# One LayerNorm application per batch in a transformer block with routed experts, the RMS factor moved into the q/k epsilon and into the copy of the values

## The chip, the cores and the metric

One Trainium2 chip, one of its cores. The metric is the device time of the program in microseconds (us); lower is better. The core has five engines that run their own instruction streams and meet at semaphores: TensorE (PE; its weight loads have rows of their own, PEld), VectorE (DVE), ScalarE (ACT), GpSimd (POOL) and SyncE (SP, which issues most transfers here).

## The reference

The input x is 8 batches of 512 tokens of 128 numbers. All is float32.

```
xn  = layernorm(x)                       # eps 1e-5
xr  = rms_norm(xn, ln1_w)                # eps 1e-6
q, k, v = xr @ Wq, xr @ Wk, xr @ Wv      # 16 heads of 8
q, k = q * rsqrt(sum(q*q) + 1e-6), same for k       # per head
a   = softmax over the later keys only of (q.k + rel_bias[bucket]) * scale
y   = (a @ v) @ Wo + xn
z   = relu(rms_norm(y, ln2_w) @ W1) @ W2 + y
x1  = x + layernorm(z)
out = x1 + layernorm(moe(layernorm(x1)))  # 8 experts, the best 2 of each token, inner size 352
```

A LayerNorm followed by an RMS norm without its weight is a LayerNorm scaled once more by a factor r of the token: xr = r * xn * ln1_w. The last token of a batch has no later key, so its attention weights are all equal and its row of a @ v is the mean of all values of the batch.

## The kernel before

The attention part runs over bodies b = 0 to 7, one for each batch, and each body has 20 positions n: four groups of four heads, five units of a group. In each position PE computes scores of a unit (`scores`, lines 684 to 694), ACT takes their exponential (`exp_unit`, line 947), and DVE or POOL multiplies them with the table of position biases (lines 414 to 422 and 1291). PE multiplies the result with the values (`pv01`, `pv23`, `pv4`, line 702). Into the same positions other work is written: the preparation of batches b+1 and b+2, and the output projection, the feed-forward layer, the norms and the routing of batches b-1 and b-2. Bodies 8 and 9 hold the rest of that work and the first expert tiles; then the expert tiles run alone, and a last stage adds and stores.

The order on each engine is written by hand. The tables `PE_AT`, `ACT_AT`, `DVE_AT` and `POOL_AT` give for each step the position at which its engine issues it, and within one position each engine's loop has a fixed order of steps. In the first dictionary of a table, a positive position of a preparing step means "in body b, for batch b+1", a negative one "in body b at position 20 + v, for batch b+2". Each engine works strictly in its order, so a step that waits holds everything behind it on its engine.

The preparation of a batch goes through one PSUM bank, M0, which has six uses per batch (`USES0 = 6`). PE fills it (`m0_full`), another engine empties it (`m0_free`), and `take0(b, k)` makes PE wait until use k-1 has been emptied:

- use 0: `pre_xt` transposes the normed x (line 618); ACT copies it to `XART` (line 953), with a sum over the tokens (`XSUM`)
- uses 1 and 2: `pre_qk` projects q and k (line 637); ACT copies them (line 959) and squares them (line 960)
- use 3: `pre_val` projects the values (line 643); ACT copies them into `V2`, which is laid out in blocks of 32 columns a head (lines 968, 969). PE at n = 1, ACT at n = 2
- uses 4 and 5: `pre_turn` transposes the normed q and k (line 650); ACT and PE split them into three bf16 parts (lines 1013 to 1021, 668), which SP sends to DRAM and reads back in the layout that `scores` needs. The first `pre_turn` stands at n = 4 on PE

Two applications of the norm are made on ACT, four instructions each (line 993): `xar` writes `XAR`, with the factor r included, for the projections (body b, n = 13, for batch b+2); `xa` writes `XA`, without it, for the residual (n = 1, for batch b-1).

DVE normalises q and k: `norm_sums` adds up the squares (line 1258) and adds the epsilon (line 1260), at n = 17 for batch b+2. `norm_roots` (lines 1266 to 1270) and `norm_apply` (line 1278) stand at n = 1, for batch b+1, and need the seeds that ACT makes at n = 1 (lines 976, 978). The order on DVE at the start of a body is: multiply of n = 19 (line 1291), `xb` (line 1552), multiply of n = 0 (line 414), the copy of the mean of values (`post(b, "vsum")`, line 1310), `norm_roots`, `norm_apply`, `post` of `o0` and `o1` (lines 1300, 1302, 1308), multiply of n = 2 (lines 421, 422), then `take_logits` (line 1336) and the routing (lines 1344 to 1357, in odd bodies only) or the multiply of n = 4 (line 1291). The order on PE is: `pv23`, `pre_val`, `vsum` (line 761), scores of n = 2, `pv4`, scores of n = 3, the transposes `rx` (line 785), `o0`, `o1` (line 758), scores of n = 4, `pv01`, `pre_turn` (line 650), `logits` (line 789), scores of n = 5, the first `peel` (line 668), `yt` (line 618) and so on. ACT has: exponentials of n = 0 and 1, seeds, `xa`, the copy `out1` (line 1027), exponential of n = 2, the two copies of values, the copy of `rx` (line 1034), exponential of n = 3, `xb2` (line 1138), exponential of n = 4, the first part (line 1013).

Of the kernel before, what the change touches and what calls it, by code (L numbers as in the profile page):

```python
# [25 lines left out]
P = 128  # L26
# [47 lines left out]
def block_kernel(nc, x_d, ln1_d, wq_d, wk_d, wv_d, rel_d, scale_d, wo_d, ln2_d, w1_d, w2_d,  # L74
# [26 lines left out]
    with ExitStack() as ctx:  # L101
# [8 lines left out]
        XA = sb("XA", [P, T, D])  # L110
# [11 lines left out]
        XAR = arena[:, WALL0 + 6656:WALL0 + 7168].rearrange("p (t c) -> p t c", t=T)  # L122
# [24 lines left out]
        XSUM = sb("XSUM", [P, NB])  # L147
# [22 lines left out]
        XBT = sb("XBT", [P, S])  # L170
# [82 lines left out]
        xar_rdy = sem("xar_rdy")  # L253
# [353 lines left out]
        def _(pe):  # L607
# [139 lines left out]
            def on_m1(body, k):  # L747
# [12 lines left out]
                elif k == "vsum":  # L760
                    mm = pe.matmul(M1[0:1, 0:P], XSUM[:, b:b + 1], WQKV[:, 2 * D:3 * D], start=True, stop=True)
# [177 lines left out]
        def _(act):  # L939
# [9 lines left out]
            def pre_copy(b, k):  # L949

                act.wait_ge(m0_full, USES0 * b + k + 1)
                if k == 0:
                    act.activation(XART[:, :], M0[:, :], ACT.Copy, accum_out=XSUM[:, b:b + 1]).then_inc(m0_free, 1)
                    return
                if k < 3:
                    if k == 1 and b >= 1:
                        act.wait_ge(ss_rdy, b)
                    ts = slice(2 * (k - 1), 2 * k)
                    act.activation(QK[:, ts, :], M0[:, :], ACT.Copy)
                    act.activation(SQ[:, ts, :], M0[:, :], ACT.Square).then_inc(m0_free, 1)  # L960
                    return
                if b == 0:
                    act.wait_ge(v2_const, 2)
                if b >= 2:
                    act.wait_ge(pv_done, 12 * (b - 1))
                v2 = V2[b % 2].rearrange("p t (n s) -> p t n s", s=64)
                v = M0[:, :].rearrange("p (t n a d) -> p t n a d", t=T, a=2, d=DH)
                act.activation(v2[:, :, :, 0:8], v[:, :, :, 0, :], ACT.Copy)
                act.activation(v2[:, :, :, 48:56], v[:, :, :, 1, :], ACT.Copy).then_inc(m0_free, 1)
# [19 lines left out]
            def norm(dst, b, r):  # L989
# [4 lines left out]
                return ins  # L994

            def xar(b):

                act.wait_ge(st_rdy, min(b, 1) + 1)
                if b > 0:
                    act.wait_ge(m0_full, USES0 * (b - 1) + 1)  # L1000
                norm(XAR, b, 1).then_inc(xar_rdy, 1)

            def xa(b):

                if b > 0:
# [75 lines left out]
            xar(1)  # L1081
# [718 lines left out]
```

## Time and profile before

| what | before |
|---|---|
| median of 3 runs | 620.87 us (619.76 to 622.0) |
| profiled execution, first to last instruction | span 616.4 us |
| what lies between them | 4.5 us, start and end of the program outside the span |
| PE busy | 528.4 us, 86% |
| ACT busy | 395.4 us, 64% |
| DVE busy | 384.0 us, 62% |
| POOL busy | 350.1 us, 57% |
| first exponential of bodies 0 to 7 at | 41.04, 77.06, 115.72, 155.76, 197.98, 240.65, 284.91, 327.74 us |

The profiled execution has no timed median of its own; its span is what the steps below are counted in, and a step that lengthens the span is taken to lengthen the median by as much. The busy shares are means over stages with different limits. A duration in a row is that of one instruction from issue to its end, and on ACT and DVE the next may start some 0.1 us before that end, so the pace is read from starts.

### The profile page before, as it was taken

The numbers are of one execution on the slowest core, as the hardware profiler recorded it, in microseconds if no ns is written. First come the engines' busy times: TensorE is split into PE (matmuls) and PEld (weight loads), VectorE is DVE, ScalarE is ACT, GpSimd is POOL, SyncE is SP. The second block draws the span as 40 slices with busy tenths as digits, with TensorE's granted clock in tenths as the row PEclk, the third lists the DMA queues.
The fourth block names the chain that finished last, engine by engine and source line by source line (L and its number), as shares of the span: only waits on it lengthen the run. The fifth ranks groups of instructions, "written<-read, shape, count | busy, mean of one in ns | idle before, by whom it ended". The sixth has DMA issues, their size and how long they took to land.

```text
span 616.4 us, 13926 instructions
## 1 busy us (share of the span) xinstructions
PE 528.4 (86%) x4585; PEld 387.8 (63%) x4585; DVE 384.0 (62%) x1089; ACT 395.4 (64%) x874; POOL 350.1 (57%) x448
## 2 busy tenths in 40 slices
PE   7868899899998899997898999989999599999170
PEld 5643455456565555654565667879899499999030
DVE  6745583965966839988658866446755335552047
ACT  3468988988878788777888783634544235554025
POOL 4023636555458875278965463764667766665535
PEclk9986999999999999999999999999999879999666
DMA  8756333203223232134546212110222122211074
GB/s 199 119 129 140 103 103 105 78 28 103 78 89 101 90 108 80 42 120 111 150 139 162 70 28 70 45 48 20 67 74 71 46 68 71 59 50 35 16 272 137
DMA packets 48118, 55.88 MB, mean 91 GB/s; under 512 B 7820, under 2 KB 42383, under 8 KB 45888
## 3 DMA queue, kind: packets, MB, share of 16 engines
q1 hardware_dynamic: 43728, 46.52, 27.7%
q0 software_dynamic: 4320, 8.47, 4.1%
q8 instruction: 39, 0.64, 0.4%
q14 instruction: 31, 0.25, 0.1%
HBM read 37.12 MB, written 18.29 MB: 90 GB/s over the span
## 4 chain that ended last, share of the span: by engine, by line
PE 42%; POOL 16%; DVE 15%; issue 11%; ACT 8%; DMA 5%; SPq 2%; DVEq 1%; POOLq 0%; ACTq 0%
PE OA L702 9%; POOL ytok L1696 8%; PE M L743 4%; PE SC L828 4%; PE M L779 3%; ACT arena L947 3%; PE SC L684 3%; POOL slots L1685 3%; POOL IDLE L1690 3%; PE OA L838 2%; PE SC L688 2%; PE M L618 2%; DVE SS L1258 2%; PE M L637 1%; PE SC L694 1%
## 5 line engine op out<-in xcount | busy, mean ns | idle before, releaser
L947 ACT ACTIVATE arena<-SC 128x1024 f32<-128x1024 f32 x160 | 161.7, 1039 | 13.3 <-PE SC L689 11.0
L828 PE MATMUL SC<-arena 128*128 128x128 f32 (+1 forms) x852 | 109.2, 279 | 0.9 <-DVE arena L1439 0.9
L828 PEld LDWEIGHTS SC<-arena 128*128 128x128 f32 (+1 forms) x852 | 101.6, 187 | 1.4 <-DVE arena L1439 1.1
L702 PE MATMUL OA<-arena 128*32 128x256 f32 (+1 forms) x1536 | 90.9, 356 | 6.7 <-DVE arena L422 2.8
L1685 POOL DMA_INDIRECT slots<-XBA,IDX x64 | 72.7, 1136 | 37.0 <-DVE IDX L1383 19.6
L1431 DVE TENSOR_TENSOR arena<-arena,SC 128x256 f32<-128x256 f32 (+1 forms) x142 | 43.5, 348 | 59.7 <-PE SC L828 49.0
L702 PEld LDWEIGHTS OA<-arena 128*32 128x32 f32 x1536 | 39.6, 110 | 46.2 <-issue 24.7
L838 PE MATMUL OA<-arena 128*128 (+1 forms) x426 | 61.1, 280 | 6.2 <-DVE arena L1431 4.2
L1696 POOL DMA_INDIRECT ytok<-YSA,XGA x39 | 40.5, 1039 | 42.9 <-POOL IDLE L1690 22.5
L421 POOL TENSOR_TENSOR arena<-arena 128x512 f32<-128x512 f32 x32 | 42.9, 1340 | 33.9 <-ACT arena L947 33.3
L838 PEld LDWEIGHTS OA<-arena 128*128 128x128 f32 (+1 forms) x426 | 54.4, 195 | 7.9 <-issue 7.9
L414 POOL TENSOR_TENSOR arena<-arena 128x512 f32<-128x512 f32 x23 | 31.2, 1358 | 45.1 <-ACT arena L947 45.1
L1044 ACT ACTIVATE arena<-SC 128x256 f32<-128x256 f32 (+1 forms) x142 | 38.6, 324 | 19.6 <-PE SC L828 14.2
L1439 DVE COPY arena<-arena 128x704 f32 x71 | 39.2, 553 | 17.4 <-issue 15.0
L1291 DVE TENSOR_TENSOR arena<-arena 128x1024 f32<-128x1024 f32 x32 | 40.3, 1261 | 14.7 <-ACT arena L947 14.7
L1696 POOL DMA_INDIRECT ytok<-arena x32 | 33.2, 1036 | 24.9 <-POOL IDLE L1690 20.2
L414 DVE TENSOR_TENSOR arena<-arena 128x512 f32<-128x512 f32 x41 | 34.1, 833 | 17.3 <-ACT arena L947 16.6
L688 PE MATMUL SC<-arena 72*128 72x384 bf16 x128 | 35.6, 332 | 7.9 <-ACT arena L947 7.9
L421 DVE TENSOR_TENSOR arena<-arena 128x512 f32<-128x512 f32 x32 | 28.3, 885 | 20.6 <-ACT arena L947 20.5
L684 PE MATMUL SC<-arena 72*128 72x512 bf16 x128 | 39.1, 388 | 1.3 <-ACT arena L947 1.3
L1050 ACT ACTIVATE YSA<-OA,XGA 128x128 f32<-128x128 f32 x39 | 14.3, 368 | 32.5 <-PE OA L838 17.7
L1662 POOL TENSOR_TENSOR arena<-arena,CF 128x512 f32<-128x512 f32 x16 | 20.3, 1286 | 22.8 <-ACT CF L1080 22.8
(238 smaller groups left out, 1073.8 us busy)
## 6 DMA issues: line engine op xcount, KB each, us to landing
arena<-parts SPq DMA_DIRECT2D x90, 192.0 KB
parts<-arena SPq DMA_DIRECT2D x16, 384.0 KB
arena<-ytok SPq DMA_DIRECT2D x8, 512.0 KB, 6.7
XGA<-slots SPq DMA_DIRECT2D x39, 65.0 KB
arena<-slots SPq DMA_DIRECT2D x32, 65.0 KB
X<-in_L_attn_x SPq DMA_DIRECT2D x4, 512.0 KB, 5.2
arena<-toe SPq DMA_DIRECT2D x16, 128.0 KB, 6.0
out<-X SPq DMA_DIRECT2D x8, 256.0 KB, 2.4
```

Of the source, the lines that this page charges most:

```text
L414: return eng.tensor_tensor(v, v, tab, ALU.mult)
L421: return [eng.tensor_tensor(a, a, TAB[:, h0:h0 + 3:2, P:3 * P], ALU.mult), eng.tensor_tensor(z, z, TAB[:, h0:h0 + 3:2, P:2 * P], ALU.mult)]
L684: mm = pe.matmul(s[:, 512 * i:512 * i + 512], KS[0:ROWS, h, 0:P], QS[0:ROWS, h, :], start=True, stop=True)
L688: pe.matmul(s[:, 512 * i:512 * i + 384], KS[0:ROWS, h, P:2 * P], QS[0:ROWS, h, P:4 * P], start=True, stop=True)
L702: mm = pe.matmul(OA[32 * j:32 * j + 32, q0:q0 + n], vals[:, t, 32 * h:32 * h + 32], probs(j), start=first, stop=last, skip_group_check=True)
L828: mm = pe.matmul(SC[0:n, r % 2, 512 * m + P * c:512 * m + P * (c + 1)], WSEL[s % 4][:, I * m + i0:I * m + i0 + n], XGT[r % 2], start=True, ...
L838: mm = pe.matmul(OA[:, 0:P], HTB[r % 2][0:n, P * c:P * (c + 1)], WALL[0:n, bass.ds(off + 2 * I + P * c, P)], start=c == 0, stop=c == NIC - 1)
L947: act.activation(EB[u], SC[:, n % 2, :], ACT.Exp).then_inc(exp_done, 1)
L1291: dve.tensor_tensor(e, e, TAB[:, heads, P:3 * P], ALU.mult).then_inc(mul_dve, 1)
L1431: ins = dve.tensor_tensor(HTB[r % 2][0:k, c0:c1], SGB[r % 2][0:k, c0:c1], SC[0:k, r % 2, 512 + c0:512 + c1], ALU.mult)
L1685: pool.indirect_dma_start(out=slots_d.ap(), out_offset=bass.IndirectOffsetOnAxis(ap=IDX[b // 2 % 2][:, k, T * r + t:T * r + t + 1], axis=0 ...
L1696: pool.indirect_dma_start(out=ytok_d.ap(), out_offset=bass.IndirectOffsetOnAxis(ap=XG[r][:, D + 1:D + 2].bitcast(I32), axis=0), in_=YS[r], ...
```

## The change

`xa` and `xar` become one step, made at the place of `xar` (n = 13, for batch b+2): ACT writes `XA[b % 3]`, without r, into one of three buffers, and both the projections and the residual read it. The projections of q, k and v are then short of the factor r. For q and k, (r q) * rsqrt(sum((r q)^2) + eps) is the same as q * rsqrt(sum(q^2) + eps / r^2), so `norm_sums` adds an epsilon of the token that `x_roots` computes (three more small DVE instructions in each of its two calls). For v, the copy from PSUM into `V2` multiplies by r; it leaves ACT and becomes the DVE step `values`, two `tensor_tensor` instructions a batch, at n = 2 of DVE's table, which in the loop is behind DVE's multiply of n = 2. The sum over tokens in `XART`'s copy goes away; the sum of the values for the last token (`vsum`) is now made by PE from `V2` with eight matmuls against a column of ones instead of one against `XSUM`. `XBT` shares the memory of `ZT`.

```
-ACT_AT = (dict(val=2, seed=1, ..., xar=-7, xa=1),
-    dict(..., xa=3))
-DVE_AT = (dict(norm0=-3, norm1=1, norm2=1, lg=2, ...
+ACT_AT = (dict(seed=1, ..., xa=-7), dict(...))
+DVE_AT = (dict(val=2, norm0=-3, norm1=1, norm2=1, lg=2, ...
...
             def pre_xt(b):
                 take0(b, 0)
-                pe.wait_ge(xar_rdy, b + 1)
-                turn4(M0, XAR).then_inc(m0_full, 1)
+                pe.wait_ge(xa_rdy, b + 1)
+                turn4(M0, XA[b % 3]).then_inc(m0_full, 1)
...
                 elif k == "vsum":
-                    mm = pe.matmul(M1[0:1, 0:P], XSUM[:, b:b + 1], WQKV[:, 2 * D:3 * D], start=True, stop=True)
+                    pe.wait_ge(m0_free, USES0 * b + 4)
+                    v = V2[b % 2].rearrange("p t (n s) -> p t n s", s=64)
+                    for t in range(T):
+                        for i, at in enumerate((0, 48)):
+                            mm = pe.matmul(M1[0:1, 64 * i:64 * i + 64], ONES[:, 0:1], v[:, t, :, at:at + DH],
+                                           start=t == 0 and i == 0, stop=t == T - 1, skip_group_check=True)
...
                 if k == 0:
-                    act.activation(XART[:, :], M0[:, :], ACT.Copy, accum_out=XSUM[:, b:b + 1]).then_inc(m0_free, 1)
+                    act.activation(XART[:, :], M0[:, :], ACT.Copy).then_inc(m0_free, 1)
                     return
...
-                act.activation(v2[:, :, :, 0:8], v[:, :, :, 0, :], ACT.Copy)
-                act.activation(v2[:, :, :, 48:56], v[:, :, :, 1, :], ACT.Copy).then_inc(m0_free, 1)
...
+            def xa(b):
+
+                act.wait_ge(st_rdy, min(b, 1) + 1)
+                if b >= 3:
+                    act.wait_ge(*drained(b - 2, "wo"))
                 for t in range(T):
                     i = T * b + t
-                    ins = act.activation(dst[:, t, :], X[:, i, :], ACT.Identity, bias=NM0[:, r, i:i + 1], scale=RSR[:, r, i:i + 1])
+                    ins = act.activation(XA[b % 3][:, t, :], X[:, i, :], ACT.Identity, bias=NM0[:, 0, i:i + 1], scale=RSR[:, 0, i:i + 1])
+                ins.then_inc(xa_rdy, 1)
...
+                link(dve.tensor_tensor(u, a, y[:, 0].unsqueeze(1).broadcast_to([P, 2, n]), ALU.mult))
+                dve.tensor_tensor(y[:, 1], y[:, 1], u[:, 0], ALU.mult)
+                link(dve.scalar_tensor_tensor(NM0[:, 1, i0:i1], u[:, 1], KQ_EPS, y[:, 0], ALU.mult, ALU.mult))
...
-                dve.tensor_scalar(SS[:, :], SS[:, :], KQ_EPS, None, ALU.add).then_inc(ss_rdy, 1)
+                ss = SS[:, :].rearrange("p (t c) -> p t c", t=T)
+                dve.tensor_tensor(ss, ss, NM0[:, 1, T * b:T * (b + 1)].unsqueeze(2).broadcast_to([P, T, 2 * H]), ALU.add
+                                  ).then_inc(ss_rdy, 1)
+
+            def values(b):
+
+                dve.wait_ge(m0_full, USES0 * b + 4)
+                if b == 0:
+                    dve.wait_ge(v2_const, 2)
+                if b >= 2:
+                    dve.wait_ge(pv_done, 12 * (b - 1))
+                v2 = V2[b % 2].rearrange("p t (n s) -> p t n s", s=64)
+                v = M0[:, :].rearrange("p (t n a d) -> p t n a d", t=T, a=2, d=DH)
+                r = RSR[:, 1, T * b:T * (b + 1)].unsqueeze(2).unsqueeze(3).broadcast_to([P, T, H // 2, DH])
+                dve.tensor_tensor(v2[:, :, :, 0:8], v[:, :, :, 0, :], r, ALU.mult)
+                dve.tensor_tensor(v2[:, :, :, 48:56], v[:, :, :, 1, :], r, ALU.mult).then_inc(m0_free, 1)
...
                     if b < NB and (n % UNITS in (0, 2, 4) or n % UNITS == 1 and takes(b, n // UNITS)):
                         dve.wait_ge(exp_done, NU * b + n + 1)
                         mul(b, n)
                     if 1 <= due(PRE["norm0"], b, n) < NB:
                         norm_sums(due(PRE["norm0"], b, n))
+                    if 1 <= due(PRE["val"], b, n) < NB:
+                        values(due(PRE["val"], b, n))
                     if 1 <= due(PRE["norm1"], b, n) < NB:
                         norm_roots(due(PRE["norm1"], b, n))
```

## Rows read from the trace of the kernel before

**Rows 1.** Busy time by engine in body 3 and in its middle; then granted clock

```profile
155.76:197.98 42.22, 39.87 (x384) 24.98 (x384) 31.06 (x88) 35.32 (x64) 25.28 (x27) 1.00 0.28 90
...
166.50:192.50 26.00, 25.96 (x248) 16.93 (x247) 17.17 (x50) 20.34 (x39) 15.25 (x16) 1.00 0.28 91
```

**Rows 2.** Chain of waits, body 3: start, us, what; first and last of 51 pieces

```profile
164.84 0.59 PE M L650 x4
...
191.29 1.07 PE M L637 x4
```

**Rows 3.** Timeline of DVE into body 3: start, us, what, idle before

```profile
155.01 1.91 DVE L1258 TENSOR_REDUCE SS<-arena 128x128 f32<-128x1024 f32 x1 [0.62 <-ACT arena L960]
...
162.36 1.43 DVE L1278 TENSOR_TENSOR arena<-arena,RSQ 128x256 f32<-128x256 f32 x4
...
166.26 0.41 DVE L422 TENSOR_TENSOR arena<-arena 128x256 f32<-128x256 f32 x1
166.60 0.17 DVE L1336 COPY LG<-M 128x32 f32<-128x32 f32 x1
```

**Rows 4.** Timeline of PE at the same place in body 3

```profile
163.76 1.07 PE L702 MATMUL OA<-arena 128*32 128x256 f32 x16
164.77 0.66 PE L650 MATMUL M<-IDN,arena 128*128 128x128 f32 x4
```

**Rows 5.** Timeline of ACT at the same place in body 3

```profile
158.16 1.64 ACT L993 ACTIVATE XA<-X,NM,RSR 128x128 f32<-128x128 f32 x4
...
160.13 0.60 ACT L1027 ACTIVATE OS<-OA 128x512 f32<-128x512 f32 x1 [0.33 <-PE OA L702]
...
161.53 0.39 ACT L968 ACTIVATE arena<-M 128x256 f32<-128x256 f32 x1
...
162.06 0.63 ACT L1034 ACTIVATE XBT<-M 128x512 f32<-128x512 f32 x1
```

**Rows 6.** Instruction groups by line: count | busy us, mean ns | idle before

```profile
L1266 DVE TENSOR_TENSOR NWA<-RSQ 128x128 f32<-128x128 f32 x8 | 2.3, 292 | 1.0 <-ACT RSQ L978 0.7
```

**Rows 7.** Timeline, PE's L650 and DVE's slot, in the first and last of six bodies

```profile
84.55 0.66 PE L650 MATMUL M<-IDN,arena 128*128 128x128 f32 x4
...
87.38 1.21 DVE L1291 TENSOR_TENSOR arena<-arena 128x1024 f32<-128x1024 f32 x1
...
295.57 0.66 PE L650 MATMUL M<-IDN,arena 128*128 128x128 f32 x4
...
297.85 0.17 DVE L1336 COPY LG<-M 128x32 f32<-128x32 f32 x1
```

**Rows 8.** Timeline of body 5: PE's output projection, and DVE's take of it

```profile
253.81 1.05 PE L770 MATMUL M<-WO,YT 128*128 128x128 f32 x8
...
256.01 0.69 DVE L1314 TENSOR_TENSOR Y<-M,XA 128x512 f32<-128x512 f32 x1
```

**Rows 9.** Timeline of PE: `vsum`, and the nearest chain of 64-column matmuls

```profile
158.57 0.38 PE L761 MATMUL M<-WQKV,XSUM 128*1 128x128 f32 x2
...
170.25 1.90 PE L795 MATMUL M<-MM,ONES 128*128 128x64 f32 x16
```

**Rows 10.** Timeline of DVE at the start of the program

```profile
16.69 1.90 DVE L1258 TENSOR_REDUCE SS<-arena 128x128 f32<-128x1024 f32 x1 [1.16 <-ACT arena L960]
...
19.57 0.29 DVE L1266 TENSOR_TENSOR NWA<-RSQ 128x128 f32<-128x128 f32 x1 [0.72 <-ACT RSQ L978]
```

**Rows 11.** Timeline of PE around its longest wait between 70 and 480 us

```profile
413.45 0.93 PE L838 MATMUL OA<-arena 128*128 x6 [2.49 <-DVE arena L1431]
...
414.33 2.64 PE L828 MATMUL SC<-arena 128*128 128x128 f32 x12
...
418.07 1.49 PE L828 MATMUL SC<-arena 128*128 128x128 f32 x12
```

**Rows 12.** Busy time by engine, as rows 1, behind two waits of PE

```profile
414.50:417.90 3.40, 3.40 (x18) 3.40 (x18) 2.14 (x7) 0.99 (x4) 2.55 (x3) 0.50 0.27 80
...
46.00:56.00 10.00, 9.86 (x66) 4.05 (x66) 7.31 (x11) 7.08 (x9) 2.51 (x2) 0.50 0.76 140
```

More of the change, by code:

```diff
@@ L46 @@
     dict(rx=0, logits=1, vsum=0, count=3, o0=1, o1=2, yt=3, wo=5, zt=6, h0=7, h1=7, h2=7, h3=7, ffn_a=8, ffn=8))
-ACT_AT = (dict(val=2, seed=1, xt=-6, qk0=-5, qk1=-2, out0=12, out1=1, rx=2, rexp=6, yt=4, ysq=12, zt=7, h0=8, h1=9, h2=10, h3=10, xb2=3, part0=4, half0=4, last0=6, part1=8, half1=9, last1=10, xar=-7, xa=1),
-    dict(out1=0, rx=0, xb2=2, rexp=3, yt=4, zt=6, ysq=6, h0=6, h1=6, h2=7, h3=7, xa=3))
-DVE_AT = (dict(norm0=-3, norm1=1, norm2=1, lg=2, top2=3, top2b=3, vsum=0, o0=1, o1=1, wo=4, ffn=13, astat=13, place=5, place2=6, tab0=6, tab1=6, tab2=9, ln=16, xstat=16, xb=19),
+ACT_AT = (dict(seed=1, xt=-6, qk0=-5, qk1=-2, out0=12, out1=1, rx=2, rexp=6, yt=4, ysq=12, zt=7, h0=8, h1=9, h2=10, h3=10, xb2=3, part0=4, half0=4, last0=6, part1=8, half1=9, last1=10, xa=-7),
+    dict(out1=0, rx=0, xb2=2, rexp=3, yt=4, zt=6, ysq=6, h0=6, h1=6, h2=7, h3=7))
+DVE_AT = (dict(val=2, norm0=-3, norm1=1, norm2=1, lg=2, top2=3, top2b=3, vsum=0, o0=1, o1=1, wo=4, ffn=13, astat=13, place=5, place2=6, tab0=6, tab1=6, tab2=9, ln=16, xstat=16, xb=19),
     dict(lg=1, top2=1, top2b=2, vsum=0, place=3, place2=3, tab0=4, tab1=17, tab2=21, o0=1, o1=2, wo=5, ffn=8, astat=9, ln=12, xstat=13, xb=15))
@@ L109, in block_kernel @@
         X = sb("X", [P, NT, D])
-        XA = sb("XA", [P, T, D])
+        XAS = sb("XAS", [P, 2, T, D])
         WALL0 = 22528
@@ L169, in block_kernel @@
         XB = [XBA[:, r] for r in range(2)]
-        XBT = sb("XBT", [P, S])
+        XBT = ZT
         R = 2 * T
@@ L952, in pre_copy @@
                 if k == 0:
-                    act.activation(XART[:, :], M0[:, :], ACT.Copy, accum_out=XSUM[:, b:b + 1]).then_inc(m0_free, 1)
+                    act.activation(XART[:, :], M0[:, :], ACT.Copy).then_inc(m0_free, 1)
                     return
[L955 to L967, printed above, removed]
-                act.activation(v2[:, :, :, 0:8], v[:, :, :, 0, :], ACT.Copy)
-                act.activation(v2[:, :, :, 48:56], v[:, :, :, 1, :], ACT.Copy).then_inc(m0_free, 1)
+                if k == 1 and b >= 1:
+                    act.wait_ge(ss_rdy, b)
+                ts = slice(2 * (k - 1), 2 * k)
+                act.activation(QK[:, ts, :], M0[:, :], ACT.Copy)
+                act.activation(SQ[:, ts, :], M0[:, :], ACT.Square).then_inc(m0_free, 1)
             def root_seeds(b):
@@ L1068, in _ @@
             x_seeds(0)
-            xar(0)
-            for k in range(4):
+            xa(0)
+            for k in range(3):
                 pre_copy(0, k)
@@ L1080, in _ @@
             act.activation(CF[:, :], CF[:, :], ACT.Exp).then_inc(tab_exp, 1)
-            xar(1)
+            xa(1)
             for k in range(2):
@@ L1110, in _ @@
                             third_part(due(PRE[f"last{m}"], b, n), m)
-                    if 2 <= due(PRE["xar"], b, n) < NB:
-                        xar(due(PRE["xar"], b, n))
+                    if 2 <= due(PRE["xa"], b, n) < NB:
+                        xa(due(PRE["xa"], b, n))
                     for k, name in enumerate(("xt", "qk0", "qk1")):
@@ L1309, in post @@
                 elif k == "vsum":
-                    dve.tensor_scalar(VROW[0:1, :], M1[0:1, 0:P], 1.0 / S, None, ALU.mult).then_inc(free1(body, k), 1)
+                    dve.tensor_scalar(VROW[0:1, :].rearrange("p (n a d) -> p a n d", a=2, d=DH),
+                                      M1[0:1, 0:P].rearrange("p (a n d) -> p a n d", a=2, d=DH), 1.0 / S, None, ALU.mult
+                                      ).then_inc(free1(body, k), 1)
                     dve.wait_ge(*drained(body, k))
@@ L1314, in post @@
                     dve.tensor_tensor(Y[:, :, :].rearrange("p t d -> p (t d)"), M1[:, :],
-                                      XA[:, :, :].rearrange("p t d -> p (t d)"), ALU.add).then_inc(free1(body, k), 1)
+                                      XA[b % 3].rearrange("p t d -> p (t d)"), ALU.add).then_inc(free1(body, k), 1)
                 elif k == "ffn":
@@ L1451, in _ @@
             norm_sums(0)
+            values(0)
             norm_roots(0)
```

24 lines of the change are left out of this document (2 added, 22 removed).

## The prediction

> **What bounds the kernel now.** I read the page's busy shares first, then the bodies one by one as stretches, then the chain of waits inside a body, and last the timelines of each engine around the place where the changed steps stand. The shares name no bound: PE 86%, ACT 64%, DVE 62%. By body they say more. In body 3, 42.22 us long, PE is busy 39.87, ACT 35.32, DVE 31.06, and from 166.5 to 192.5 us PE is busy in 25.96 of 26.00 us [rows 1]. The chain of waits says the same: from the first `pre_turn` (line 650) to the q projection (line 637) it runs on PE alone, in 51 pieces without a wait for another engine [rows 2]. Only around the boundary of two bodies does it leave PE, for ACT (exponentials and copies). So a body is a PE-bound stretch of some 27 us, and a boundary of some 13 us in which ACT, DVE and PE wait for each other. Work taken from ACT can only count in the boundary; a delay put in front of PE's `pre_turn` counts in full.
>
> At the boundary DVE is the fullest engine. In body 3 its row starts at 155.01, on ACT's last square, and runs without idle time past 166.60 [rows 3]. PE meanwhile reaches its first `pre_turn` at 164.77, right behind `pv01` [rows 4]. Before the change that is no conflict: `pre_turn` needs the normed q and k, which DVE has finished at 163.8, four instructions from 162.36 [rows 3], and the free bank, which ACT has emptied with its two copies (line 968 at 161.53, the next step at 162.06) [rows 5].
>
> **What leaves ACT.** The four instructions of `xa` take 1.64 us, of which the next may overlap 0.1; the two copies 0.53 (161.53 to 162.06) [rows 5]. The accumulator read I leave at nothing. That is 2.1 us a body, 15 us in seven bodies, and 1.5 more in body 8. I count it at nothing. With `xa` in place ACT already waits 0.33 us for PE's `pv4` before it copies `OS` [rows 5]; without `xa` it waits 1.9. The two copies let `XBT` start 0.53 us earlier, but what follows from that (the transposes `o1`, then DVE's `post`) ends in DVE's queue, which is full. In the middle of the body PE is the bound [rows 1].
>
> **What is added on DVE, and where.** `values` is two `tensor_tensor` of 128x256 float32 from PSUM. No such row exists; the nearest is line 1278, the same size from SBUF, four of them in 1.43 us, so 0.34 each in sequence, with 0.41 for one alone like line 422 [rows 3]. Two take 0.34 + 0.41 = 0.75 us to the end of the second. Bounds 0.6 and 1.1. The epsilon as `tensor_tensor` costs like line 1266, 0.29 us [rows 6]; the instruction that it replaces has as many elements and cannot take less than half of that, so +0.06 is taken of at most +0.15. So DVE's queue gets 0.74 us longer, and `pre_turn` sees the end of `values` 0.75 + 0.06 and about 0.1 us for the semaphore after the slot in which it starts: 0.9.
>
> The VectorE page of the Trainium skill (VectorE: DVE Perf Modes, the perf-mode tier table) gives `tensor_tensor` in float32 one element per cycle from either memory; by its formula for the operation, 256 elements make an estimated 0.42 us each, and the sum stays.
>
> The slot decides. In DVE's order `values` stands at n = 2 behind the multiply of n = 2, and with that behind the roots, `norm_apply`, the posts of `o0` and `o1` and lines 421 and 422. It is the third use of M0, and `pre_turn`, the fourth, now waits for it through `take0(b, 4)`. In body 3 line 422 gives way at 166.60 [rows 3]; `values` ends at 167.5, and `pre_turn` starts there instead of at 164.77 [rows 4]: 2.7 us later. Everything behind it on PE is held: `logits`, scores of n = 5, `peel`, `yt`, then `wo` and all of the PE-bound stretch. ACT waits for the transposed q in its first part, with the exponential of n = 5 behind it. PE leaves no slack until line 637, so the delay reaches the next boundary whole.
>
> The same difference, from the same two rows in each body plus 0.9: body 1, 87.38 + 0.9 - 84.55 = 3.7, of which 0.5 was already spent waiting for `yt` further on, so 3.2; body 6, 297.85 + 0.9 - 295.57 = 3.2 [rows 7]. Bodies 2 and 5 are like 3, 2.7 each; body 4 is like 6, 3.2. In body 5 DVE is the bound further on: it takes `wo` at 256.01 although PE's projection ended near 254.9 [rows 8]. Of the 2.7 us only 254.9 + 2.7 - 256.01 = 1.6 arrive. Body 0 waits for the bias table anyway, and body 7 prepares nothing. Sum: 3.2 + 2.7 + 2.7 + 3.2 + 1.6 + 3.2 = 16.6 us. Bounds: with 0.6 for `values` and 0.5 us regained per body at `XBT`, 13; with 1.1 and nothing lost in body 5, 19.7.
>
> **vsum.** Eight float32 matmuls are 16 instructions (one is two in the trace). The present pair with one column of weights takes 0.38 us for 128 columns, 0.11 apart; sixteen of 64 columns with full weights take 1.90, 0.11 apart [rows 9]. With one column of weights and half the columns I take 0.055 each: 0.9 us instead of 0.2, +0.65; bounds +0.5 and +1.6. In bodies 1 to 7 it ends before PE's new wait and costs nothing (if that wait were gone it would be in front of `pv4` and cost its 0.65 each). In body 8 nothing covers it: +0.65.
>
> **Start.** `values(0)`, 0.75 us, falls into the 0.72 us in which DVE waits for ACT's seeds; the three new instructions of `x_roots` are smaller than line 1266's 0.29 [rows 6], so under 0.9 us in the first call, and DVE waits 1.16 us soon after [rows 10]. Zero; bounds 0 and 1. `XBT` in `ZT`'s memory adds no wait: `ZT` is written after `logits` has read `XBT`, and read before the next `rx`.
>
> **PE's clock.** The stall leaves PE idle. In body 3 `pv01` ends at 164.83 [rows 4], `pre_turn` starts at 167.5: 2.6 us idle; in bodies 1, 4 and 6 3.2 to 3.7. The trace has PE idle for 2.49 us before 413.45 [rows 11], and the stretch behind it runs at a granted clock of 0.50, 1.2 GHz instead of 2.4; so does the stretch from 46 us on [rows 12]. Behind the shorter waits of body 3 the clock stays at 1.00 [rows 1]. At half clock twelve matmuls of line 828 took 2.64 us, at full clock 1.49 [rows 11]: 1.15 us lost, and at most 1.7 in 3.4 us of pure PE work. I take 1.5 for a fall, and four falls (three of the long gaps, one of the three short ones): 6 us. Bounds: none, and all six at 1.7, 10; if some last 10 us as from 46 us on [rows 12], 5 each.
>
> The Trainium skill says that waits between bursts bring PE back to half rate, each time anew (TensorE: Matmul & The Clock Gate, HAM oscillation). By that all six boundaries fall and the time is the upper end of the forecast case; the rows agree for gaps of 2.5 us.
>
> **Sum.** 16.6 + 0.65 + 6 = 23.3 us on a span of 616.4, about 640; the median lies 4.5 us above the span, so 620.87 + 23.3 = 644.
>
> **Rivals.**
> - The stall without any fall of the clock: 620.87 + 17.3 = 638. For it: the idle gaps of bodies 2, 3 and 5 are hardly longer than the shortest that was followed by a fall. Chance 0.17.
> - The stall with longer stretches at half clock, as from 46 us on: three of 10 us would make 620.87 + 17.3 + 15 = 653, more of them past 655. Against it: behind the gap at 413 only 3.4 us were slow. Chance 0.10.
> - Faster: ACT is the bound after all and its order, not DVE's queue, releases PE. Then 2.2 us a body and 1.5 at the end go: 620.87 - 16.6 = 604. For it: ACT is busy 35.3 of 42.2 us [rows 1]. Against it: its 0.33 us wait for PE right behind `xa` [rows 5]. It decides only if `values` gets to run before 164.8 in body 3, two microseconds ahead of its slot. Chance 0.05.
> - The stall is absorbed: DVE catches up by what `post` no longer waits for, and only `vsum` remains, 0.65 in eight bodies at most: 621 to 626. Against it: DVE has no idle time to give. Chance 0.08, of which 0.03 within 0.3%.
>
> The forecast case, stall and three to six falls, 640 to 648, has 0.60; 644 is taken. The range 634 to 654 holds it, the first rival and half of the second. Faster by over 0.3% 0.05, within 0.3% (about what a measurement here can tell) 0.03, slower 0.92.
>
> **What the profile after would show.** Line 650 on PE with an idle time of 2.6 to 3.7 us before it, released by DVE's `values`, in bodies 1 to 6; the exponential of n = 5 that much later; the other intervals between exponentials as before; ACT some 16 us less busy. Half clock right behind the stalls. `vsum` with 16 instructions in 0.9 us. The prediction is wrong if DVE runs `values` ahead of lines 421 and 422, or if PE's idle time sits before another line.

## The result and the profile after

The changed kernel takes 646.34 us (median of 4 runs, 643.56 to 648.84), the kernel before 620.51 on the same chip: ratio 1.0412, 95% interval 1.0375 to 1.0449. It is slower by 26 us; 644 was forecast. Its profiled execution is the slowest of the four, 648.84 us with a span of 647.1.

The page of the changed kernel: its span, its busy shares, and the granted clock in 40 slices.

```profile
span 647.1 us, 14123 instructions
...
PE 546.3 (84%) x4697; PEld 401.0 (62%) x4697; DVE 389.5 (60%) x1111; ACT 379.7 (59%) x818; POOL 348.0 (54%) x448
...
PEclk9986979989989969989979999999989969999666
```

ACT has 15.7 us less work, as the removed steps cost, and the time is still 30.7 us longer than the span before. The row of the clock has dips all along the bodies. To place the loss, take the first exponential (line 950 here) of bodies 0 to 7: 40.75, 79.17, 123.40, 167.74, 214.03, 262.53, 311.72, 359.32 us. Against before, body 0 is 2.4 us longer, bodies 1 to 6 take 280.15 instead of 250.68 (29.5 more), body 7 from its first to its last exponential takes 41.94 against 41.95, and all that follows is 0.9 shorter. So the loss lies in bodies 1 to 6, which prepare a batch. Body 0's 2.4 us can't be counted to it: experiments 5 and 10 below are one kernel, and their two profiled executions have 36.68 and 39.59 us for body 0.

Body 3 by engine (columns as in [rows 1]), then a stretch each of bodies 3, 2 and 4.

```profile
167.74:214.03 46.29, 41.74 (x398) 26.30 (x398) 34.87 (x90) 33.37 (x58) 26.10 (x27) 0.96 0.25 81
...
181.50:184.90 3.40, 3.40 (x32) 1.63 (x31) 3.06 (x14) 3.03 (x4) 0.00 (x0) 0.53 0.00 0
137.10:140.50 3.40, 3.40 (x31) 1.67 (x29) 0.85 (x1) 3.03 (x4) 0.06 (x1) 0.54 0.00 0
225.90:236.10 10.20, 8.93 (x52) 6.32 (x53) 2.54 (x6) 4.22 (x6) 6.29 (x6) 0.51 0.09 29
```

PE is busy in 41.74 of 46.29 us, before in 39.87 of 42.22. Timeline of DVE in body 3, to be laid beside [rows 3].

```profile
172.86 0.27 DVE L1305 TENSOR_SCALAR VROW<-M 1x128 f32<-1x128 f32 x1
...
174.40 1.43 DVE L1273 TENSOR_TENSOR arena<-arena,RSQ 128x256 f32<-128x256 f32 x4
...
177.77 0.67 DVE L419 TENSOR_TENSOR arena<-arena 128x512 f32<-128x512 f32 x1
178.37 0.41 DVE L420 TENSOR_TENSOR arena<-arena 128x256 f32<-128x256 f32 x1
178.70 0.41 DVE L1254 TENSOR_TENSOR arena<-M,RSR 128x256 f32<-128x256 f32 x1
179.04 0.40 DVE L1255 TENSOR_TENSOR arena<-M,RSR 128x256 f32<-128x256 f32 x1
```

Timeline of PE at the same place, beside [rows 4].

```profile
175.88 1.07 PE L700 MATMUL OA<-arena 128*32 128x256 f32 x16
179.50 0.66 PE L648 MATMUL M<-IDN,arena 128*128 128x128 f32 x4 [2.55 <-DVE arena L1255]
```

Timeline of ACT at the same place, beside [rows 5].

```profile
172.79 0.60 ACT L1010 ACTIVATE OS<-OA 128x512 f32<-128x512 f32 x1 [2.55 <-PE OA L700]
...
180.19 0.60 ACT L996 ACTIVATE arena<-M 128x512 bf16<-128x512 f32 x1 [3.05 <-PE M L648]
```

`values` (lines 1254, 1255) runs without idle time behind the multiply of n = 2, ends at 179.44, and `pre_turn` (line 648) starts 0.06 us later, with PE idle for 2.55 us. The normed q and k that it turns were ready at 175.83. The chain of waits there has DVE on it where before it stayed on PE [rows 2].

```profile
178.44 0.34 DVE arena L420
178.77 0.33 DVE arena L1254
179.11 0.34 DVE arena L1255
179.45 0.04 issue
179.50 0.66 PE M L648 x4
```

PE is idle before line 648 for 3.01, 2.54, 2.55, 3.02, 2.55 and 3.02 us in bodies 1 to 6, and for 3.52 us in body 0. Half clock follows each of the six: 3.4 us long in bodies 2 and 3, 6.8 in bodies 1, 5 and 6, 10.2 in body 4; 37.4 us in the six bodies, against none there before. The groups of the changed kernel, where [rows 6] has one of before:

```profile
L648 PE MATMUL M<-IDN,arena 128*128 128x128 f32 x64 | 12.8, 334 | 20.8 <-DVE arena L1255 20.2 <-DVE arena L1273 0.3 <-ACT arena L1004 0.2
L763 PE MATMUL M<-arena,ONES 128*1 128x64 f32 x128 | 8.4, 219 | 0.0
L1254 DVE TENSOR_TENSOR arena<-M,RSR 128x256 f32<-128x256 f32 x8 | 3.3, 407 | 0.0
...
L1261 DVE TENSOR_TENSOR NWA<-RSQ 128x128 f32<-128x128 f32 x8 | 3.2, 401 | 0.4
L1241 DVE TENSOR_TENSOR SS<-SS,NM 128x128 f32<-128x128 f32 x8 | 2.7, 335 | 0.3
```

Of the 20.8 us that PE waits before line 648, 20.2 end with `values` (seven waits, body 0's with them): the time sits on one edge of the program.

### The profile page after: what moved, and what is told of

It reads as the page before. It is cut to its first block, busy times and chain, and to the rows that moved or that the text cites. A ratio compares the mean times of both kernels' runs of the same rounds, so it can differ in the third digit from the quotient of the medians.

```text
span 647.1 us, 14123 instructions
## 1 busy us (share of the span) xinstructions
PE 546.3 (84%) x4697; PEld 401.0 (62%) x4697; DVE 389.5 (60%) x1111; ACT 379.7 (59%) x818; POOL 348.0 (54%) x448
## 4 chain that ended last, share of the span: by engine, by line
PE 43%; DVE 20%; POOL 13%; issue 9%; ACT 6%; DMA 5%; SPq 2%; DVEq 1%; POOLq 0%; ACTq 0%
PE OA L700 8%; POOL ytok L1696 7%; PE SC L831 5%; PE M L782 4%; PE M L741 4%; PE SC L682 3%; PE OA L841 3%; ACT arena L950 3%; POOL IDLE L1690 2%; DVE SS L1238 2%; PE M L616 2%; PE SC L686 2%; POOL slots L1685 2%; DVE arena L1273 2%; DVE XBA L1552 2%
## 5 line engine op out<-in xcount | busy, mean ns | idle before, releaser
L700 PE MATMUL OA<-arena 128*32 128x256 f32 (+1 forms) x1536 | 95.7, 371 | 2.5 <-DVE arena L420 2.5
L1685 POOL DMA_INDIRECT slots<-XBA,IDX x64 | 68.9, 1077 | 44.6 <-DVE IDX L1380 27.2
L700 PEld LDWEIGHTS OA<-arena 128*32 128x32 f32 x1536 | 41.3, 115 | 46.1 <-issue 26.8
L682 PE MATMUL SC<-arena 72*128 72x512 bf16 x128 | 43.6, 427 | 3.1 <-ACT arena L950 1.5
L412 DVE TENSOR_TENSOR arena<-arena 128x512 f32<-128x512 f32 x41 | 33.1, 810 | 14.3 <-ACT arena L950 14.1
L419 DVE TENSOR_TENSOR arena<-arena 128x512 f32<-128x512 f32 x32 | 27.4, 858 | 23.2 <-ACT arena L950 23.1
L1662 POOL TENSOR_TENSOR arena<-arena,CF 128x512 f32<-128x512 f32 x16 | 22.1, 1398 | 23.3 <-ACT CF L1063 23.3
```

Source lines behind the costliest of these rows:

```text
L412: return eng.tensor_tensor(v, v, tab, ALU.mult)
L419: return [eng.tensor_tensor(a, a, TAB[:, h0:h0 + 3:2, P:3 * P], ALU.mult), eng.tensor_tensor(z, z, TAB[:, h0:h0 + 3:2, P:2 * P], ALU.mult)]
L682: mm = pe.matmul(s[:, 512 * i:512 * i + 512], KS[0:ROWS, h, 0:P], QS[0:ROWS, h, :], start=True, stop=True)
L700: mm = pe.matmul(OA[32 * j:32 * j + 32, q0:q0 + n], vals[:, t, 32 * h:32 * h + 32], probs(j), start=first, stop=last, skip_group_check=True)
L1685: pool.indirect_dma_start(out=slots_d.ap(), out_offset=bass.IndirectOffsetOnAxis(ap=IDX[b // 2 % 2][:, k, T * r + t:T * r + t + 1], axis=0 ...
```

## The experiments

Twelve kernels ran, in four groups (1 to 4, 5 to 7, 8 to 10, 11 and 12); each group has its own runs of the kernel before (medians 619.77, 620.50, 620.57, 622.22 us), and each ratio is to those.

**1. Values ahead of the roots.** If the slot is the cause, moving `values` to the front of n = 1 removes stall and half clock.

```
-DVE_AT = (dict(val=2, norm0=-3, norm1=1, ...
+DVE_AT = (dict(val=1, norm0=-3, norm1=1, ...
```

> The changed kernel with one number moved: the step `values` on DVE at n = 1 instead of n = 2, so that it stands ahead of the roots and `norm_apply`, behind the multiply of n = 0 and the mean of values, and no longer behind the posts and the multiply of n = 2. Theory (the stall is the place of `values` in DVE's queue): DVE reaches it at about the time at which PE's `pv4` is done, so it waits little; the free bank is there before PE comes to the first `pre_turn`, which then waits at most for `norm_apply`, later by the 0.7 us of `values`. PE's idle time before that line falls from 2.5 to 3.0 us to under 0.7, the granted clock stays at 1.00 through bodies 1 to 6, and the time is that of the kernel before within 1%: 616 to 627 us. Rival A (it is the work added to DVE, 0.75 us a batch, in a queue that is full, wherever it stands): no more than half of the 26 us comes back, 630 us or more. Rival B (it is the longer `vsum` or the ScalarE work that moved): unchanged, 640 to 649 us.

Measured 636.39 us, ratio 1.0242 (1.0198 to 1.0287): more than half of the loss stays, a miss; the time lies in the range of rival A (the work costs wherever it stands), which experiment 5 then rules out. DVE, POOL and PE in body 3:

```profile
169.07 2.52 DVE L1273 TENSOR_TENSOR arena<-arena,RSQ 128x256 f32<-128x256 f32 x4
...
169.81 1.49 POOL L419 TENSOR_TENSOR arena<-arena 128x512 f32<-128x512 f32 x1 [4.32 <-ACT arena L950]
...
171.73 0.63 PE L648 MATMUL M<-IDN,arena 128*128 128x128 f32 x4 [0.77 <-DVE arena L1273]
```

`norm_apply` took 2.52 us instead of 1.43. In the seven batches behind the first it took 2.5 to 3.75. Beside it runs POOL's multiply of n = 3, which it had just escaped before; the 0.75 us that `values` puts in front pushes it under that. PE still waits 2.56 us before line 648 in bodies 4 and 6, and there is half clock in bodies 3 to 6, 20.5 us in sum. So there is a second cost at this place: time on DVE that depends on what POOL does. The Trainium skill has POOL's SBUF interfaces shared with VectorE, with contention for instructions that have two SBUF inputs (GPSIMD Engine Reference, Specifications); `norm_apply` is one, and its rows here agree.

**2. Values on ACT again.** The rest of the change stays; ACT copies the values at n = 2 as before, without the factor r, so this kernel's attention output is not the reference's.

```
-ACT_AT = (dict(seed=1, ...
+ACT_AT = (dict(val=2, seed=1, ...
-DVE_AT = (dict(val=2, norm0=-3, ...
+DVE_AT = (dict(norm0=-3, ...
...
+                act.activation(v2[:, :, :, 0:8], v[:, :, :, 0, :], ACT.Copy)
+                act.activation(v2[:, :, :, 48:56], v[:, :, :, 1, :], ACT.Copy).then_inc(m0_free, 1)
```

> The changed kernel with the copy of the values back on ACT at n = 2, two instructions as before the change; the factor r is left out of the values, since an ACT copy of that shape has no operand for it. All else of the change stays: one norm application, the epsilon as a `tensor_tensor`, the longer `vsum`. Theory (the place of `values` alone makes the loss, and the rest is worth little): PE does not wait before its first `pre_turn`, no half clock in bodies 1 to 6, and the time is within 3 us of the kernel before, 617 to 624 us. Rival A (ACT was a bound, and `xa`, 1.5 us a body, was on the path): clearly faster than the kernel before, 605 to 612 us. Rival B (`vsum` or the epsilon carries a good part of the loss): 628 us or more.

Measured 623.14, ratio 1.0061 (1.0044 to 1.0078), as expected. The intervals between the exponentials of n = 4 and 5 are 3.03 and 3.93 us, no longer than before. All but 0.6% hangs on `values` being on DVE at n = 2. The single application, the epsilon and `vsum` together gain nothing, though ACT is spared the four instructions of `xa` in each body. Experiment 3 has the same longer `vsum` and keeps `xa`: its bodies 1 to 6 take 253.42 us, here 253.33, so `xa` is worth nothing there.

**3. vsum alone**, put into the kernel before, with its 16 instructions.

```
-                    mm = pe.matmul(M1[0:1, 0:P], XSUM[:, b:b + 1], WQKV[:, 2 * D:3 * D], start=True, stop=True)
+                    pe.wait_ge(m0_free, USES0 * b + 4)
+                    ...
+                            mm = pe.matmul(M1[0:1, 64 * i:64 * i + 64], ONES[:, 0:1], v[:, t, :, at:at + DH], ...)
```

> The kernel before with one part of the change: `vsum` made from the values in V2 by eight matmuls against a column of ones. Theory: sixteen instructions take 0.9 us instead of 0.2, in front of `pv4`, which ACT and then PE wait for at the start of a body; with no other stall to hide it, 0.3 to 0.65 us a body in seven or eight bodies, 623 to 626 us. Rival A (the boundary is DVE's, and the cost is hidden as in the changed kernel): within 1 us of the kernel before. Rival B (with full-width weight loads 0.11 us an instruction): 1.6 us a body, 630 us or more.

Measured 624.8, ratio 1.0083 (1.0063 to 1.0103), as expected. One of its four runs took 1617.18 us; the median of the other three is 624.04. The interval from n = 1 to 2 grows from 3.95 to 4.62 in bodies 1, 2, 3 and 5. So `vsum` is not free by itself. In the changed kernel DVE's row in body 3 has no idle time between 166.99 us and the end of `values` at 179.44, so the stall hides it.

**4. PE kept busy in the stall.** This separates the stall from the clock: 5 or 6 matmuls without use fill PE's idle time in front of the first `pre_turn` of bodies 1 to 6, in a part of a bank that is written again before it is read. They must not delay `pre_turn` themselves.

```
+                            take1(b, nxt)
+                            for _ in range(6 if b in (1, 4, 6) else 5):
+                                pe.matmul(bank1(b, nxt)[:, 2 * P:4 * P], IDN[:, :], ..., start=True, stop=True)
```

> The changed kernel with PE kept busy while it waits: before the first `pre_turn` of bodies 1 to 6, five matmuls of 256 columns on constants (six in bodies 1, 4 and 6), 0.45 us each, into the half of a bank of M1 that is free then and written over later. The stall stays, only its idle time is filled. Theory (the loss is the stall, 16 to 17 us, and the fall of TensorE's clock behind it, 8 to 11): the granted clock stays at 1.00 from body 1 to body 7, and the time is 634 to 639 us. Rival A (the clock costs nothing, since PE is not the bound behind the stall): unchanged, 643 us or more. Rival B (the clock is most of the loss): below 630 us.

Measured 632.74, ratio 1.0221 (1.0196 to 1.0245), 1.3 us below the expected range. Timeline of PE in body 3, then the six bodies as a stretch, of this kernel and of the changed one.

```profile
172.42 2.42 PE L913 MATMUL M<-IDN 128*128 128x256 f32 x10
175.05 0.66 PE L648 MATMUL M<-IDN,arena 128*128 128x128 f32 x4 [0.20 <-DVE arena L1261]
```

```profile
78.65:342.80 264.15, 247.25 (x2368) 157.68 (x2380) 185.28 (x471) 196.90 (x334) 154.62 (x149) 1.00 0.30 91
```

```profile
79.17:359.32 280.15, 250.00 (x2314) 154.58 (x2314) 186.88 (x471) 198.04 (x335) 154.58 (x149) 0.93 0.27 86
```

The clock is 1.00 over the whole stretch, and 264.15 - 250.68 = 13.5 us of loss are left: the stall by itself. The other 280.15 - 264.15 = 16.0 us of the profiled execution is the clock. The profiled execution of the changed kernel is its slowest. By medians the two kernels differ by 646.34 - 632.74 = 13.6 us, by their ratios (1.0412 and 1.0221) by 11.9, so the clock is worth 12 to 16. From n = 4 to 5 the bodies now take 3.08, 2.60, 2.60, 3.09, 2.60 and 3.10 us more than before.

**5 and 10. Values behind norm_apply.** Experiment 1 said that the slot must be early and must not push `norm_apply`. Here `values` is called directly behind it.

```
-                    if 1 <= due(PRE["val"], b, n) < NB:      # was behind mul(b, n)
-                        values(due(PRE["val"], b, n))
...
                     if 1 <= due(PRE["norm2"], b, n) < NB:
...
+                    if 1 <= due(PRE["val"], b, n) < NB:
+                        values(due(PRE["val"], b, n))
```

> The changed kernel with `values` on DVE at n = 1 directly behind `norm_apply`, in front of the posts of `o0` and `o1`. Theory (in the run with `values` first, DVE's `norm_apply` came 0.7 us later, into POOL's multiply of n = 3, and took 2.5 to 3.8 us instead of 1.4; so the place decides twice, by PE's wait for the bank and by what DVE meets on POOL): `norm_apply` keeps its old time and its 1.4 us, `values` ends about when PE comes to the first `pre_turn`, no wait of over 1.3 us before it, the granted clock stays at 1.00 through bodies 1 to 6, and what is left of the loss is `vsum`: 621 to 626 us. Rival (0.75 us more in DVE's full queue costs as much wherever it stands, by delaying posts and `yt`): 630 us or more.

> The run with `values` behind `norm_apply` once more, on the same chip as the run with `vsum` behind `pv4`, so that the two can be told apart: 619 to 622 us, within 0.3% of the kernel before.

Measured 620.69, ratio 1.001 (0.9992 to 1.0028), 0.3 us below the expected range; and in the repetition 622.6, ratio 1.0018 (0.999 to 1.0046). Both agree with the kernel before. DVE and PE in body 4 of experiment 5:

```profile
208.10 1.43 DVE L1273 TENSOR_TENSOR arena<-arena,RSQ 128x256 f32<-128x256 f32 x4
...
209.79 0.41 DVE L1255 TENSOR_TENSOR arena<-M,RSR 128x256 f32<-128x256 f32 x1
...
210.25 0.66 PE L648 MATMUL M<-IDN,arena 128*128 128x128 f32 x4 [0.16 <-issue]
```

The same work on the same engine, in another slot, and the 26 us are gone.

**6. vsum at n = 0** instead of n = 1, on top of experiment 5.

```
-PE_AT = (dict(..., vsum=1, ...
+PE_AT = (dict(..., vsum=0, ...
```

> As the run with `values` behind `norm_apply`, and `vsum` on PE at n = 0 instead of n = 1. Theory: `vsum` takes 1.0 us of PE's time ahead of `pv4` in either place, which ACT's copy and the exponential of n = 2 wait for, so only the part that falls into PE's waits at n = 0 and 1 (0.2 to 0.9 us a body) comes back: 1 to 3 us less than that run, 619 to 624 us. Rival (PE's order at the boundary is free, and all of `vsum` can be hidden): 616 to 619 us, faster than the kernel before.

Measured 623.2, ratio 1.0037 (1.0006 to 1.0068): within the stated range, but the 1 to 3 us of gain did not come. The median is 2.5 us above that of experiment 5, but the two intervals overlap, and bodies 1 to 6 take 252.34 us in the one trace and 252.30 in the other. The interval from n = 1 to 2 did fall, to 3.63, but `vsum` now stands between the two scores in front of the exponential of n = 1, where PE had waited only 0.23 us (1.52 from n = 0 to 1 instead of 0.92), and n = 4 to 5 grew from 3.97 to 4.36.

**7. Factor r in the application, residual scaled back.** The kernel before with one application that includes r; ACT's copies of the values and the old `vsum` and epsilon stay, and DVE adds the residual with 1/r, in four instructions instead of one.

```
-  dve.tensor_tensor(Y[...], M1[:, :], XA[...], ALU.add)
+  for t in range(T):
+      last = dve.scalar_tensor_tensor(Y[:, t, :], XA[b % 3][:, t, :], NM0[:, 0, T * b + t:T * b + t + 1],
+                                      M1[:, P * t:P * (t + 1)], ALU.mult, ALU.add)
```

> The kernel before with one norm application made the other way round: ACT writes only the version with r (at n = 13, three buffers), the projections, the copies of the values, the epsilon and `vsum` stay as they were, and the residual is taken back to the version without r on DVE, by four `scalar_tensor_tensor` instructions with 1/r in place of one `tensor_tensor` (+0.4 us a batch at n = 4). Theory (taking `xa` from ACT is worth little, since ACT then waits for PE's `pv4`, and the loss comes only from `values` and `vsum`): no wait of PE before the first `pre_turn`, within 2 us of the kernel before, 617 to 622 us. Rival (1.5 us a body of ACT work at the boundary is worth most of its time): 606 to 612 us. Other rival (four instructions in place of one push DVE into POOL's multiplies): 624 us or more.

Measured 626.26, ratio 1.0088 (1.006 to 1.0116): a miss for the theory, as its rival had it. DVE and POOL in body 4:

```profile
219.24 1.12 DVE L1302 SCALAR_TENSOR_TENSOR Y<-XAS,NM,M 128x128 f32<-128x128 f32 x4 [4.26 <-PE M L769]
220.28 2.12 DVE L413 TENSOR_TENSOR arena<-arena 128x512 f32<-128x512 f32 x1
...
220.56 1.28 POOL L413 TENSOR_TENSOR arena<-arena 128x512 f32<-128x512 f32 x1
```

The longer residual shifts DVE's multiply (0.67 us alone) under POOL's, where it took 2.12 us, and from n = 6 to 7 bodies 4 and 6 take 4.19 us instead of 1.65.

**8. vsum at n = 2**, behind `pv4`, on top of experiment 5, to take its 0.67 us away from the front.

```
-PE_AT = (dict(..., vsum=1, ...
+PE_AT = (dict(..., vsum=2, ...
```

> As the run with `values` behind `norm_apply`, and `vsum` on PE at n = 2 instead of n = 1, behind `pv4` in place of ahead of it. Its result is needed only by DVE's copy of the mean, which DVE reaches over 1 us later. Theory (the 0.7 us that `vsum` gained counts because it stands ahead of `pv4`, which ACT's copy and the exponential of n = 2 wait for): the interval between the exponentials of n = 1 and n = 2 goes back from 4.6 to 3.9 us or less; of the 0.7 us some returns at n = 3, whose scores then stand behind `vsum`: 1 to 3 us less than the run with `values` behind `norm_apply`, 617 to 620 us. Rival (the time of `vsum` counts on PE wherever it stands, as in the run with it at n = 0): no difference within 1 us.

Measured 628.97, ratio 1.0128 (1.0094 to 1.0162): a miss by 9 us. The interval from n = 1 to 2 fell to 3.53 as foreseen. The exponential of n = 3 then came earlier, with it POOL's multiply, and that met `norm_apply` again, which took 2.51 to 3.05 us in bodies 1, 2, 3 and 5. PE waited 1.3 to 2.5 us before line 648. Body 3, DVE and POOL:

```profile
168.84 2.51 DVE L1273 TENSOR_TENSOR arena<-arena,RSQ 128x256 f32<-128x256 f32 x4
...
169.57 1.50 POOL L419 TENSOR_TENSOR arena<-arena 128x512 f32<-128x512 f32 x1 [3.65 <-ACT arena L950]
```

**9. Values alone.** The kernel before with nothing changed but that DVE copies the values (two `tensor_copy`, at n = 2).

```
-                act.activation(v2[:, :, :, 0:8], v[:, :, :, 0, :], ACT.Copy)
-                act.activation(v2[:, :, :, 48:56], v[:, :, :, 1, :], ACT.Copy).then_inc(m0_free, 1)
+                dve.tensor_copy(v2[:, :, :, 0:8], v[:, :, :, 0, :])
+                dve.tensor_copy(v2[:, :, :, 48:56], v[:, :, :, 1, :]).then_inc(m0_free, 1)
```

> The kernel before with one part of the change: the copy of the values on DVE at n = 2, behind the multiply of n = 2, as two plain copies; ACT's `xa` and `xar`, the epsilon and `vsum` stay. Theory: the place of this copy alone makes nearly the whole loss; PE waits 2.5 to 3.7 us before the first `pre_turn` of bodies 1 to 6, the clock falls behind each wait, and the time is 638 to 649 us. Rival (it needs the longer `vsum` or the missing `xa` beside it): 622 to 634 us.

Measured 649.35, ratio 1.047 (1.0421 to 1.0519): the whole loss, and 3 us more, 0.35 above the expected range. This one edit is enough for it. It loses more than the changed kernel because ACT's copies are gone while `vsum` is still short: the exponential of n = 3 comes 0.5 us earlier than in the kernel before and 0.7 earlier than in the changed one, POOL's multiply reaches `norm_apply` (2.52 us in bodies 2, 3 and 5), and PE waits 4.07 us there instead of 2.55. In the changed kernel the longer `vsum` keeps the two apart: `norm_apply` ends at 175.83 and POOL's multiply starts at 175.79.

**11 and 12. The test of that reading.** If experiment 8 fails because POOL comes too early, an ACT step put in front of the exponential of n = 3, which then comes 0.5 us later, must undo it; the control has the same step in experiment 5, where it should do nothing.

```
-ACT_AT = (dict(..., xb2=3, ...
+ACT_AT = (dict(..., xb2=2, ...
```

> As the run with `vsum` behind `pv4` and `values` behind `norm_apply`, with one number moved: ACT's copy `xb2`, 0.5 us, at n = 2 instead of n = 3, so ahead of the exponential of n = 3 instead of behind it. In that run `norm_apply` took 2.5 us instead of 1.4 in bodies 2 and 3, with POOL's multiply of n = 3 beginning 0.7 us after it; the multiply waits for the exponential of n = 3. Theory (DVE's two-input instruction on SBUF data is held while POOL's multiply runs, so an engine that gets faster can pull POOL's work onto DVE's): with the exponential 0.5 us later `norm_apply` takes 1.4 to 1.9 us in bodies 2, 3 and 5, PE's wait before the first `pre_turn` falls from 1.3 us to under 0.9, and the time falls by 1 to 3 us, to 625 to 628 us; body 1, which has no `xb2`, keeps its wait of 2.5 us. Rival (the order of `vsum` and the scores holds PE, not DVE's slow instruction): unchanged or slower.

> The control: the run with `values` behind `norm_apply` and `vsum` at its place, with `xb2` at n = 2. There `norm_apply` takes 1.4 us already, so there is nothing to win; the exponential of n = 3 comes 0.5 us later and the one of n = 4 at its old time. Theory: within 0.3% of the kernel before, 619 to 623 us. Rival (the later exponential of n = 3 delays POOL's multiply and with it PE's `pv23`): 624 us or more.

Measured 626.28, ratio 1.0092 (1.0062 to 1.0123), and 622.55, ratio 1.0018 (0.9985 to 1.0051), both as expected. In body 3 of the first, DVE and POOL:

```profile
167.06 1.43 DVE L1273 TENSOR_TENSOR arena<-arena,RSQ 128x256 f32<-128x256 f32 x4
...
168.30 1.34 POOL L419 TENSOR_TENSOR arena<-arena 128x512 f32<-128x512 f32 x1 [4.16 <-ACT arena L950]
```

Delaying an exponential made `norm_apply` 1.1 us faster in bodies 2, 3 and 5; in body 1 it still took 3.05. The medians of 8 and 11, 628.97 and 626.28, are from different groups; by their ratios the intervals touch (1.0094 to 1.0123), so the gain in time is likely and not settled, while the durations in the two traces are plain.

## Why the prediction was right

**What left ACT, counted at nothing.** Right. ACT is 15.7 us less busy and waits instead: 2.55 us before `OS`. Experiments 2, 5 and 12 have relief of ACT without the stall, and none is faster than the kernel before; for `xa` alone the pair of experiments 2 and 3 shows it. What it said of "the other intervals between exponentials as before" did not hold: in body 3 the one from n = 1 to 2 is 4.62 instead of 3.95, by `vsum`, and the next 1.39 instead of 1.91, since the two copies are gone; the two nearly cancel. In the rival "Faster", 2.2 us in seven bodies and 1.5 are 16.9, not 16.6, which leaves its 604.

**The slot and the wait.** Right in every body that it named: line 648 is released by `values`, which runs where DVE's table has it. The price of the two instructions was 0.74 from the start of the first to the end of the second, 0.75 forecast (0.40 to 0.42 each; the prediction's estimate of 0.42 from the VectorE page of the Trainium skill agrees); `pre_turn` followed after 0.06, 0.1 taken; the epsilon is an instruction of 0.29 in place of 0.23, +0.06 as taken. Stalls of 3.08, 2.60, 2.60, 3.09, 2.60 and 3.10 us were measured with the clock held up, against 3.2, 2.7, 2.7, 3.2 and, before what body 5 regains, 2.7, and 3.2.

**What of the stall arrives: 16.6 forecast, 13.5 measured.** "PE leaves no slack until line 637, so the delay reaches the next boundary whole" was too strict. With the clock held up bodies 1 to 6 are 3.18, 2.76, 2.48, 1.50, 2.05 and 1.49 us longer. In bodies 4 and 6 the interval behind n = 9 shrank from 3.42 and 3.44 to 2.62: PE had an idle time of 0.92 us before line 702 there, which the delay used up. Body 5 regained 0.5 of its 2.6 in the same interval (3.13 to 2.62), not 1.1 at `wo`.

**The clock: 6 us forecast, 12 to 16 measured.** This is the term that was mis-sized, beyond its upper bound of 10, and its rival "longer stretches at half clock" was nearer in mechanism. Two parts of it failed. "Four falls" were six: idle times of 2.54 and 2.55 us were followed by a fall each time. (The section that the prediction cites from the Trainium skill, HAM oscillation in TensorE: Matmul & The Clock Gate, speaks of longer waits than these, so that all six would fall did not follow from it; the rows show it.) And "1.5 for a fall", read from the one fall of 3.4 us among the expert tiles [rows 11], holds for bodies 2 and 3 alone (1.56 and 1.57 by the difference to experiment 4); where the half clock lasted 6.8 or 10.2 us it cost 2.38, 4.34, 2.88 and 3.28. The rival had priced 10 us at 5, which is about what body 4 shows. Too little for the clock and too much for the stall cancel in part: 22.6 forecast for both, 29.5 in the profiled execution, which is the slowest of four. So the mechanism was right, and that 644 came within 2.4 us of the median is in part luck.

**vsum.** 16 instructions took 1.05 us in the changed kernel, so +0.67 for +0.65, and cost nothing in bodies 1 to 7, as far as the trace of body 3 and the length of body 7 show. "If that wait were gone it would be in front of `pv4` and cost its 0.65 each" came true in part in experiment 3: 1.67, 0.68 and 0.41 us in bodies 1 to 3, nothing in 4 to 6.

**Start and body 0.** "Body 0 waits for the bias table anyway" is not settled. PE waited 3.52 us for `values` there and the body is 2.4 us longer, but it is 2.9 and 2.5 us longer than before in experiments 2 and 3 too, where `values` is not on DVE, and only 1.1 in experiment 9, where PE waited 4.06 us. No cost of the start shows: the first exponential is at 40.75, before it was at 41.04, and in the traces of the experiments it lies between 39.2 and 41.7.

**Span and median.** "The median lies 4.5 us above the span" compared one execution's span with the median of others. In every run of these studies the time lies 1.7 us above its own span, so 2.8 of the 4.5 were the difference between executions. The sum of the steps, 23.3 us, was put on the median and stands against 646.34 - 620.51 = 25.8 us.

**What stays open.** Why the half clock lasts 3.4 us behind one stall and 10.2 behind another of the same length was not tried apart. Nor is it known whether body 0's 2.4 us come from the change.

## What to carry to other kernels

A step moved to another engine costs by its slot in that engine's queue and by who waits for the buffer that it frees, not by its duration: 0.74 us of DVE work cost 26 us in one slot and nothing three microseconds further forward. Before choosing the slot, look at what the third engine does then, because a shift of 0.5 us can put an instruction under another one's memory traffic. And reckon with an idle time of PE of some 2.5 us twice, once as a wait and once as the clock behind it: in bodies 1 to 6 of the changed kernel that held six times of six.

## What the runs showed of the hardware

- DVE's `tensor_tensor` with both inputs in SBUF slows down beside POOL's `tensor_tensor`: four of 128x256 took 1.43 us alone and 2.51 to 3.75 us beside POOL's multiply of 128x512 (1.3 to 1.5 us); in the longer ones POOL's 128x256 multiply behind it, and in the longest an indirect transfer too, fell into the same time. A 128x512 one took 2.12 instead of 0.67. The two of `values`, with one input in PSUM, took 0.40 to 0.42 us on average in every kernel in which they ran, in body 3 of experiment 5 too, where they ran at 165.15 to 165.90 us beside POOL's multiply of 165.19 to 166.47.
- In the changed kernel the granted clock fell to half behind each idle time of PE of 2.54 to 3.02 us in bodies 1 to 6, but not behind one of 2.31 us that ended at 445.51 us. Shorter ones were sometimes followed by a fall: 0.77 us in body 3 and 1.60 us in body 5 of experiment 1, 1.60 us in experiment 10, 1.36 us in experiment 8. The last, in body 5, and the stretch 2.8 us later:

```profile
258.74 0.66 PE L648 MATMUL M<-IDN,arena 128*128 128x128 f32 x4 [1.36 <-DVE arena L1255]
```

```profile
261.50:264.90 3.40, 3.40 (x31) 1.60 (x30) 2.99 (x16) 2.81 (x4) 0.00 (x0) 0.54 0.01 2
```

  The same idle time in bodies 2 and 3 of that trace was not followed by a fall, nor was one of 2.00 us in body 1 of experiment 1. And in body 5 of experiment 11 the clock fell at 264.0 us although PE had been idle for no longer than 0.43 us at a time in the 8 us before:

```profile
264.10:267.40 3.30, 3.30 (x14) 2.37 (x14) 2.89 (x17) 2.49 (x4) 1.06 (x1) 0.50 0.00 0
```

  So the length of the last idle time alone does not say whether the clock falls.

- A float32 matmul with one column of weights and 64 columns started 0.056 us behind the one before it (16 in 1.05 us to the end of the last), against the 0.11 of the same columns with full weights [rows 9].
